# The third filter of a two-layer graph kernel on the split parts of the ring: twelve fp32r products for four in fp32

## The reference, cut to what matters

```python
h = relu(A @ (x @ W1) + b1)
h = relu(A @ (h @ W2) + b2)
x = layernorm(x + h)
A2 = A @ A; A3 = A2 @ A
f1 = A @ x @ V1; f2 = A2 @ x @ V2; f3 = A3 @ x @ V3
x = layernorm(x + (f1 + f2 + f3) / 3)
```

## Time and profile before

| | |
|---|---|
| median of 3 runs | 255.85 us (255.49 to 256.27) |
| the profiled execution's own time | 255.64 us |
| its span, first to last instruction | 253.8 us |
| TensorE busy | 246.8 us (97%), 1152 matmul records |
| DVE busy | 201.2 us (79%) |
| ACT busy | 192.3 us (76%) |
| moved by DMA | 20.49 MB, most of it in the first 50 us |

### The profile page before, as it was taken

The page is one execution under the profiler, slowest core; times in us unless marked ns, Lnnn a source line. Parts: engine busy times, 40 slices in busy tenths (PEclk is TensorE's granted clock), DMA queues, the critical chain, the costliest instruction groups (busy, mean ns, idle before and its releaser), DMA issues.

```text
span 253.8 us, 3754 instructions
## 1 busy us (share of the span) xinstructions
PE 246.8 (97%) x1152; PEld 204.1 (80%) x1152; DVE 201.2 (79%) x391; ACT 192.3 (76%) x335; POOL 17.0 (7%) x25
## 2 busy tenths in 40 slices
PE   8999999999999999999999999999999999999991
PEld 8688788888888888877888888888888888888881
DVE  0897899796788989898678877767676767889855
ACT  3997998886868787978877787867677777788750
POOL 1000000000003121130000000000000000303033
PEclk9999999999999999999999999999999999999999
DMA  6999999920000000000000000000000000010111
GB/s 229 394 386 385 387 386 387 400 80 0 3 0 3 0 0 3 0 0 1 0 4 0 0 0 3 0 0 1 4 0 0 0 3 0 0 43 0 45 39 45
DMA packets 11252, 20.49 MB, mean 81 GB/s; under 512 B 1248, under 2 KB 2144, under 8 KB 11104
## 3 DMA queue, kind: packets, MB, share of 16 engines
q1 hardware_dynamic: 10944, 19.93, 21.4%
q10 hardware_dynamic: 288, 0.33, 0.4%
HBM read 19.20 MB, written 1.05 MB: 80 GB/s over the span
## 4 chain that ended last, share of the span: by engine, by line
PE 83%; SPq 5%; DMA 4%; DVE 3%; ACT 2%; issue 2%; POOL 1%; POOLq 0%; ACTq 0%; DVEq 0%
PE filters L387 17%; PE filters L380 17%; PE filters L381 17%; PE pair L387 9%; PE pair L380 9%; PE pair L381 9%; DMA adj<-a_t 4%; SPq L266 3%; PE weighted L355 2%; PE turned L357 2%; ACT ring_high L517 2%; DVE ring_low L627 1%; SPq L264 1%; SPq L270 1%; POOL rstd L315 1%
## 5 line engine op out<-in xcount | busy, mean ns | idle before, releaser
L627 DVE TENSOR_TENSOR ring_low<-adj,ring_high 128x512 fp32r<-128x512 f32 x240 | 160.0, 688 | 34.6 <-ACT ring_high L517 31.7
L517 ACT ACTIVATE ring_high<-adj 128x512 fp32r<-128x512 f32 x240 | 148.6, 629 | 32.4 <-PE filters L381 16.4
L380 PE MATMUL filters<-ring_high,operand_low 128*128 128x512 f32 x156 | 62.0, 398 | 0.0
L387 PE MATMUL filters<-ring_low,operand_high 128*128 128x512 f32 x156 | 61.2, 392 | 0.3 <-DVE ring_low L627 0.2
L381 PE MATMUL filters<-ring_high,operand_high 128*128 128x512 f32 x156 | 60.8, 389 | 0.0
L387 PEld LDWEIGHTS filters<-ring_low,operand_high 128*128 128x128 f32 x156 | 29.3, 188 | 7.8 <-DVE ring_low L627 1.5
L381 PEld LDWEIGHTS filters<-ring_high,operand_high 128*128 128x128 f32 x156 | 29.3, 188 | 5.7
L380 PEld LDWEIGHTS filters<-ring_high,operand_low 128*128 128x128 f32 x156 | 29.3, 188 | 5.7
L380 PE MATMUL pair<-ring_high,operand_low 128*128 128x512 f32 x84 | 33.3, 396 | 0.0
L387 PE MATMUL pair<-ring_low,operand_high 128*128 128x512 f32 x84 | 33.0, 393 | 0.2
L381 PE MATMUL pair<-ring_high,operand_high 128*128 128x512 f32 x84 | 32.7, 390 | 0.0
(11 more groups left out here) (82 smaller groups left out, 208.4 us busy)
## 6 DMA issues: line engine op xcount, KB each, us to landing
adj<-a_t SPq DMA_DIRECT2D x48, 256.0 KB, 9.7
resident_raw<-a_t SPq DMA_DIRECT2D x16, 256.0 KB, 9.7
nodes<-x_rows SPq DMA_DIRECT2D x1, 1024.0 KB, 11.6
lead<-lead_in SPq DMA_DIRECT2D x3, 256.0 KB, 4.3
out_rows<-nodes SPq DMA_DIRECT2D x3, 256.0 KB, 2.4
lead<-lead_in ACTq DMA_DIRECT2D x1, 192.0 KB, 3.0
lead<-lead_in SPq DMA_DIRECT2D x1, 128.0 KB, 2.7
lift_raw<-lifts SPq DMA_DIRECT2D x1, 128.0 KB, 11.3
```

What stands on the lines that cost most here:

```text
L380: nc.tensor.matmul(bank, y_low, a_high, start=first, stop=False)
L387: used = nc.tensor.matmul(bank, y_high, a_low, start=False, stop=last)
L517: nc.scalar.activation(ring_high[:, n % RING, :], source, ACT.Copy).then_inc(high_ready, 1)
L627: nc.vector.tensor_tensor(ring_low[:, n % RING, :], source, ring_high[:, n % RING, :].bitcast(F32), ALU.subtract).then_inc(low_ready, 1)
```

## The change

The post of hop 3 and its evacuation go. In the wide step of hop 3, behind the three products with V2, TensorE multiplies the four 128-column parts of the same ring item by V3: high part x V3's low part, high x high, low x high, each as a product of 128 columns in fp32r with the part of the ring as stationary side, into `weighted`. V3 moves from `params` to `lifts` and is split with V1 and V2. The ring's slot is given back behind the last of these twelve products. ACT's `operand_tiles` for hop 3 comes when TensorE has passed the wide step and waits for `low_used` of that item; DVE's comes an item later, as before. The counts on `chunk_evacuated` and `post_multiplied` leave out hop 3.

```diff
+THIRD = 2
-V3 = B2 + 1
-PARAMS = V3 + D
+PARAMS = B2 + 1
 def post_step(hop, c):
+    if hop == 3:
+        return STEPS.index((hop, c, WIDE)) + 1
     return end_of(hop, c) + (8 if (hop, c) == (2, 1) else 4)
+def item_of(hop, c):
+    return BEFORE[STEPS.index((hop, c, WIDE))]
 def evacuations(n):
-    return [(hop, c) for hop in range(HOPS) for c in range(CHUNKS)
+    return [(hop, c) for hop in (0, 1, 2, 4) for c in range(CHUNKS)
...
-        lift_high = sb("lift_high", [P, len(LIFTS), D], F32R)
+        lift_high = sb("lift_high", [P, THIRD + 1, D], F32R)
...
+        def evacuated(hop, c):
+            return (hop - (hop > 3)) * CHUNKS + c + 1
...
-                    sp.dma_start(par[:, W2:V3], params[:, W2:V3]).then_inc(layer_0_in, 16)
+                    sp.dma_start(par[:], params[:]).then_inc(layer_0_in, 16)
...
-            sp.dma_start(par[:, V3:], params[:, V3:]).then_inc(layer_1_in, 16)
...
             def post(hop, c):
-                pe.wait_ge(chunk_evacuated, hop * CHUNKS + c + 1)
+                pe.wait_ge(chunk_evacuated, evacuated(hop, c))
...
-                    if hop in (0, 3):
-                        w = V3 if hop else W2
-                        last = nc.tensor.matmul(weighted[:, t, :], tile, par[:, w:w + D], start=True, stop=True)
+                    if hop == 0:
+                        last = nc.tensor.matmul(weighted[:, t, :], tile, par[:, W2:W2 + D], start=True, stop=True)
...
+            def third_filter(bank, second_high, c, n):
+                z_high, z_low = ring_high[:, n % RING, :], ring_low[:, n % RING, :]
+                w_high, w_low = lift_high[:, THIRD, :], lift_low[:, THIRD, :]
+                pe.wait_ge(low_ready, n + 1)
+                nc.tensor.matmul(bank, second_high, z_low, start=False, stop=False)
+                bank_free(3, c)
+                for t in range(TPC):
+                    part = slice(t * P, (t + 1) * P)
+                    nc.tensor.matmul(weighted[:, t, :], z_high[:, part], w_low, start=True, stop=False)
+                    high = nc.tensor.matmul(weighted[:, t, :], z_high[:, part], w_high, start=False, stop=False)
+                    low = nc.tensor.matmul(weighted[:, t, :], z_low[:, part], w_high, start=False, stop=True)
+                    if t == TPC - 1:
+                        high.then_inc(high_used, 1)
+                        low.then_inc(low_used, 1)
...
                 used = nc.tensor.matmul(bank, y_high, a_high, start=False, stop=False)
+                if hop == 3 and k == WIDE:
+                    third_filter(bank, y_high, c, n)
+                    return
...
-                    act.wait_ge(post_multiplied, hop * CHUNKS + c + 1)
+                    if hop == 3:
+                        act.wait_ge(low_used, item_of(hop, c) + 1)
+                    else:
+                        act.wait_ge(post_multiplied, evacuated(hop, c))
```

More of the change, by code:

```diff
@@ L158, in graph_layers @@
         par = sb("par", [P, PARAMS])
-        lift_high = sb("lift_high", [P, len(LIFTS), D], F32R)
-        lift_raw = nc.alloc_sbuf_tensor_at("lift_raw", [P, len(LIFTS), D], F32, offset=place[0])
-        lift_low = sb("lift_low", [P, len(LIFTS), D], F32R)
+        lift_high = sb("lift_high", [P, THIRD + 1, D], F32R)
+        lift_raw = nc.alloc_sbuf_tensor_at("lift_raw", [P, THIRD + 1, D], F32, offset=place[0])
+        lift_low = sb("lift_low", [P, THIRD + 1, D], F32R)
         ident = sb("ident", [P, P])
@@ L182, in graph_layers @@
         lifts_in = sem("lifts_in")
-        layer_1_in = sem("layer_1_in")
         warm_ready = sem("warm_ready")
@@ L342, in post @@
             def post(hop, c):
-                pe.wait_ge(chunk_evacuated, hop * CHUNKS + c + 1)
+                pe.wait_ge(chunk_evacuated, evacuated(hop, c))
                 if (hop, c) == (1, 0):
                     pe.wait_ge(ident_ready, 1)
-                elif (hop, c) == (3, 0):
-                    pe.wait_ge(layer_1_in, 16)
                 elif (hop, c) == (0, 0):
@@ L408, in _ @@
                     for chunk in range(CHUNKS):
-                        if (h, chunk) != (HOPS - 1, CHUNKS - 1) and post_step(h, chunk) == at:
+                        if (h, chunk) != (HOPS - 1, CHUNKS - 1) and h != 3 and post_step(h, chunk) == at:
                             post(h, chunk)
@@ L429, in _ @@
             nc.tensor.matmul(last_banks[2], ident[:], nodes[:, TILES - 2, :], start=True, stop=False)
-            pe.wait_ge(chunk_evacuated, HOPS * CHUNKS)
+            pe.wait_ge(chunk_evacuated, evacuated(HOPS - 1, CHUNKS - 1))
             add_sums(0)
@@ L433, in _ @@
             nc.tensor.matmul(last_banks[3], ident[:], nodes[:, TILES - 1, :], start=True, stop=False)
-            pe.wait_ge(chunk_evacuated, HOPS * CHUNKS + 1)
+            pe.wait_ge(chunk_evacuated, evacuated(HOPS - 1, CHUNKS - 1) + 1)
             add_sums(2)
@@ L443, in evacuate @@
                 if hop or c:
-                    act.wait_ge(post_multiplied, hop * CHUNKS + c)
+                    act.wait_ge(post_multiplied, evacuated(hop, c) - 1)
                 if hop < 2:
@@ L526, in _ @@
             act.wait_ge(chunk_summed, HOPS * CHUNKS)
-            act.wait_ge(post_multiplied, HOPS * CHUNKS - 1)
+            act.wait_ge(post_multiplied, evacuated(HOPS - 1, CHUNKS - 2))
             for half in range(HALVES):
@@ L538, in residual @@
                 group = nodes[:, c * TPC:(c + 1) * TPC, :]
-                dve.wait_ge(post_multiplied, hop * CHUNKS + c + 1)
+                dve.wait_ge(post_multiplied, evacuated(hop, c))
                 if (hop, c) == (1, 0):
@@ L640, in _ @@
             for half in range(HALVES):
-                dve.wait_ge(post_multiplied, HOPS * CHUNKS + half)
+                dve.wait_ge(post_multiplied, evacuated(HOPS - 1, CHUNKS - 2) + half + 1)
                 norm_stats(hop, c, half, last_banks[halves[half]])
@@ L662 @@
         "params": np.concatenate([np.asarray(L0_gnn_W2), np.asarray(L0_gnn_b1)[:, None],
-                                  np.asarray(L0_gnn_b2)[:, None], np.asarray(L1_gnn_W3)], axis=1),
-        "lifts": np.stack([np.asarray(L1_gnn_W1), np.asarray(L1_gnn_W2)], axis=1),
+                                  np.asarray(L0_gnn_b2)[:, None]], axis=1),
+        "lifts": np.stack([np.asarray(L1_gnn_W1), np.asarray(L1_gnn_W2), np.asarray(L1_gnn_W3)], axis=1),
     }
```

## The result

The changed kernel takes 257.89 us (median of 6 runs, 257.48 to 258.16), the kernel before 255.91 (6 runs, 255.49 to 256.27): the ratio is 1.0077, 95% interval 1.0064 to 1.0091, some 2.0 us slower. The forecast was 257.6.

The account below looks back on a forecast made before the run. The prediction took TensorE, busy 97% of the span, to bound the kernel. Added 5.36 less removed 3.57 made +1.8 us: 257.4 from the profiled 255.64, forecast 257.6 as the median is 0.2 higher; range 256.9 to 263.3.

Parts of the forecast that it names:

- (a): TensorE, hop 3: four plain fp32 groups of 0.89 us each go, 3.57 us in all.
- (d): TensorE, hop 3: 48 added products at 0.112 us each, 1.34 us a chunk, 5.36 us in all.
- (b): ACT, hop 3: four evacuations into chunk_t go, 0.60 us each, 2.4 us; gain costed at nothing.
- (c): SP: one 64 KB transfer goes into that of the lifts; gain nothing.
- (e): Lift split on ACT and DVE: three matrices for two, at most 0.2 us more each, once; cost zero.
- (f): Third filter moves from after tile 3 of the next chunk to the wide step, after tile 4; nothing added.
- (g): Ring slot of the wide item is freed 1.34 us later; least slack 1.3 us, nothing added.
- R1: Rival for the added products: a narrow one costs as much as 512 columns, 0.227 us; 263.2 us; chance 0.21.
- R2: Rival for the added products: short load and product don't overlap, 0.168 us each; 260.3 us; chance 0.10.
- R3: Rival: the ring runs dry after the third filter; 258.8 us, at most 262.7; chance 0.08.
- R4: Rival for the added products: quicker loads, 0.057 us a product; 255.0 us, 0.3% faster; chance 0.05.
- R5: Rival for the added products: a step midway, 0.085 us a product; 256.4 us; chance 0.06.

Follow-up runs that it names:

- e1 to e4: The changed kernel with the twelve products' load or moving columns cut or widened, four runs: 255.49, 258.33, 258.13 and 258.19 us.
- e6: The changed kernel with its twelve fp32r products put back to four plain fp32 ones at the same place: 256.08 us, ratio 1.0012 to the kernel before.
- e8: The kernel before with only hop 3's post moved behind the wide step: 255.82 us, ratio 1.0000.
- e7: The changed kernel with each of the twelve products made twice: 263.10 us, ratio 1.0289 to the kernel before.
- e1: The changed kernel with the twelve products' loads cut from 128 to 64 columns, moving side kept at 128: 255.49 us, one run.
- e10: The kernel before with the loads of hop 3's four plain fp32 products cut to 64 columns: 257.14 us, one run.
- e11: The kernel before with the moving side of hop 3's four plain fp32 products cut to 64 columns: 255.86 us, one run.

## Why the prediction was right

By its own steps. **(a), (d)** were the whole of it. The group was to go from 0.89 to 1.34 us and did; four of them make +1.8, and the stretch shows 1.78. The step of 0.112 rested on two starts 0.11 apart; e1 to e4 show that the reading, a load that can't be hidden, is the right one. The medians differ by 2.0, of which 0.2 is outside the stretch and within what runs vary. With the 0.06 by which before's median rose from three runs to six, that is about the 0.3 by which 257.6 fell short of 257.89.

**(b), (c)** ACT's 2.4 us and SP's transfer bought nothing: e6 has both and is not faster than before. **(e)** The lift split grew to 507 ns on ACT and 549 ns on DVE, 0.11 and 0.13 each where I allowed up to 0.2, and TensorE didn't wait. **(f)** e8 shows the place to cost nothing. **(g)** The late release is real, 1.47 us of ACT's idle time a chunk, and hidden; e7 shows that 2.8 us would be hidden as well.

The rivals: **R1** (0.227 for a narrow product, 263.2 us) was the largest part of my doubt (0.21 of 0.50) and is wrong in kind. What 0.223 for a whole fp32 product showed was two records, each with a load of 0.11 and a stream of 0.11, not a floor for narrow products. **R2** (no overlap, 0.168) is refuted by 0.112. **R3** fell with e7. **R4** and **R5** (0.057 and 0.085) had the product itself nearly right, it steps at 0.060 in e1, but it was never the bound. The 81 ns of the Trainium skill ("TensorE: Matmul & The Clock Gate", "Back-to-back issue gap") isn't reached by these fp32r products, 0.112. The Trainium skill's rule on loads on the same page, in "LDWEIGHTS (loading the stationary operand)", time by columns, 107 ns for 128, agrees with 0.112; the 0.060 for 64 columns in e1 is no more than an upper bound for the load, as the product's stream may set it.

## What to carry to other kernels

Price a short matmul by the larger of its load and its stream. In fp32r the two meet at about 256 moving columns for a load of 128 (0.112 at 192 and below, 0.118 at 256), so four plain fp32 products (eight loads) are cheaper than twelve fp32r products of 128 columns, and the work that fp32r saves is only saved where the moving side is wide. If the stationary side must be the data, put more matrices side by side on the moving side until it has 256 columns, before adding loads. Relieving an engine with a quarter of its time free is worth nothing while TensorE never waits.

## What the runs showed of the hardware that I had not expected

A product of 256 moving columns costs 0.118 us and one of 64 costs 0.112, if a load of 128 columns is behind each. A load of 64 columns takes at most 0.060 us in fp32r, but in fp32 (e10) the same narrowing made the group longer, 1.22 us for 0.89, with 0.35 and 0.17 us of idle time on the load side about it. A plain fp32 product of 128 x 128 x 128 takes 0.223 us, two records that step at 0.11 whether the load (e10) or the stream (e11) is halved.
